# Ending the dense expert steps ahead of the first slot transposes in a two-layer kernel

## The chip, the cores and the metric

The kernel runs on one core of one Trainium2 chip. The metric is the device time of one execution in microseconds (us). A core has TensorE (matrix products), VectorE, ScalarE, GpSimd and SyncE (issues DMAs), each with its own stream of instructions, which meet in semaphores. In the rows PE is TensorE, DVE is VectorE, ACT is ScalarE, POOL is GpSimd, SP is SyncE.

## The reference, cut to what matters

Two layers, each with an attention block and a mixture of experts, are applied to 16 x 64 tokens of 128 channels. The change lies in the last block, the experts of the second layer: 1024 tokens, 8 experts of width 512, the two best experts for each token:

```python
logits = xf @ router_w.T
top_vals, top_idx = jax.lax.top_k(logits, TOP_K)          # TOP_K = 2, E = 8
gate = jax.nn.softmax(top_vals)
comb = zeros((N, E)).at[arange(N)[:, None], top_idx].add(gate)
for e in range(E):
    h = jax.nn.gelu(xf @ w1[e].T, approximate=False)
    out = out + comb[:, e:e + 1] * (h @ w2[e].T)
```

## The kernel before

The kernel is written engine by engine, with semaphores set and awaited by hand; each engine runs its instructions in the order written. In the experts of the second layer the first half of the tokens (512) is computed densely: every expert for every token, weighted afterwards. The second half is computed sparsely: each token's row is scattered by an indirect DMA of GpSimd into a DRAM buffer `slots_x`, sorted by expert, in 15 slots of 128 rows; the slots are read back in four batches (0: slots 0 to 2, 1: slots 3 to 6, then 7 to 10, 11 to 14), and each slot is multiplied with the weights of the one expert that owns it. Values are split in a high and a low 16-bit part, so that each product is made of three.

All of it is one loop of 47 steps (`STEPS`), n = 0 to 46. Steps 0 to 27 are dense (`DENSE` = 28: expert e = n // 4, quarter c = n % 4 of its width, for experts 0 to 6), steps 28 to 42 are the 15 slots, and 43 to 46 are the dense steps of expert 7. A step goes through five stages:

- up(n), on TensorE, into one of four PSUM banks: `up1` (lines 1585 to 1587, three products of 512 columns) for a dense step, `slot_up` (lines 1659 to 1661, four times three products of 128 columns) for a slot. The slot's expert is a register value, so the addresses of its weights are computed by register operations of TensorE.
- gelu(n) (line 782) and high(n) (line 787, the high part), on ScalarE: `gelu_step` and `high1_step`.
- low(n) (line 1208, the low part), on VectorE: `low1_step`.
- down(n), on TensorE: `down1` (lines 1606 to 1608, four times three products) or `slot_down` (lines 1678 and 1679, four times two).

TensorE computes up(n + 3) in the iteration of down(n). For n = 25 and above the four parts of a slot's up stand between the four parts of down. Every engine runs the loop in its own way: ScalarE does gelu(n + 1), then high(n); VectorE does low(n), then, at every fourth n, `add_expert` (line 1217), which weighs a finished dense expert's sum and adds it to the residual. add_expert(5) stands in iteration 24 and add_expert(6) in iteration 28. From iteration 29 on `result_row` (line 1231) takes the result of each slot, and GpSimd scatters it to `slots_y` (line 587).

Before a slot's up, its rows have to be turned: `transpose_slots(b)` (line 1640) has TensorE transpose a batch into PSUM bank 5, two 128 x 128 pieces a slot, once the batch has been read (`in_slots[b]`), and `copy_slots(b)` (line 1225) has VectorE copy that to `xsT`. `slot_up_waits(i)` waits for that copy. The table `FETCH` says in which iteration both stand: batch 0 in 24, batch 1 in 27, batch 2 in 31, batch 3 in 35. In the rows the tile `xsT` and the result rows go by the name of the buffer that holds them, `kM`; the slots' rows as read are in `kS`, and the hidden values are in `attention_or_experts`.

Of the kernel before, what the change touches and what calls it, by code (L numbers as in the profile page):

```python
# [43 lines left out]
FC = 4  # L44
# [11 lines left out]
SLOTS = 15  # L56
ROW = 264
AFTER = FC
DENSE = X1 * FC - AFTER
STEPS = DENSE + SLOTS + AFTER  # L60
FETCH = {DENSE - 4: 0, DENSE - 1: 1, DENSE + 3: 2, DENSE + 7: 3}

PACK = {}
_at = 0
# [7 lines left out]
def build_program(nc, x, ctx_t, ctx_v, pack, rows, w_first, w_second, qkvo, causal, ident_h, ident_b, sel_first, sel_second, out):  # L72
    with ExitStack() as stack:
# [178 lines left out]
        def reached(count):  # L252

            return max(count, 0) if type(count) is int else count
# [43 lines left out]
        def up_bank(n):  # L298

            return bank((3, 2, 0, 1)[n % 4])  # L300
# [38 lines left out]
        def gt(g):  # L339
            return slice(g * TG, (g + 1) * TG)  # L340
# [251 lines left out]
        def _(a):  # L592
# [48 lines left out]
            for c in range(4):  # L641
# [4 lines left out]
                n = min(4, NB - 1 - 4 * c)  # L646
# [132 lines left out]
            def gelu_step(n):  # L779

                a.wait_ge(s["mm1b"], n + 1)
                a.activation(up_bank(n), up_bank(n), ACT.Gelu, scale=1 / (XS * XS)).then_inc(s["gelu"], 1)  # L782

            def high1_step(n):
                a.wait_ge(s["gelu"], n + 1)
                a.wait_ge(s["mm2b"], reached(n - 3))
                a.activation(ehi[:, n % 4, :], up_bank(n), ACT.Copy, scale=HS).then_inc(s["hhi1"], 1)  # L787

            gelu_step(0)
            for n in range(STEPS):  # L790
                if n + 1 < STEPS:
                    gelu_step(n + 1)
                high1_step(n)
                if n < 2:
                    copy_pT(7, n)
                if n == 1:
                    gate_tanh(0)
                if n == 3:
                    copy_two_oT()
                if n == 5:  # L800
                    copy_oT(7)
                if n == 11:
                    copy_xT(3, 1, 5)
                if n == 12:
                    a.wait_ge(s["s1"], NT)
                    a.activation(xrow[:, :, :, 0:P], xn[:, gt(1), :].unsqueeze(2).to_broadcast([P, TG, 2, P]), ACT.Copy, scale=XS)\
                        .then_inc(s["rows_hi"], 1)
                if n == 16:
                    gate_tanh(1)
# [10 lines left out]
        def _(v):  # L820
# [413 lines left out]
            for n in range(STEPS):  # L1234
# [33 lines left out]
                if n == 22:  # L1268
                    place_gates()
                if n in FETCH:  # L1270
                    copy_slots(FETCH[n])
            def add_slots(k, t):
# [15 lines left out]
        def _(pe):  # L1288
# [92 lines left out]
            for g in range(G):  # L1381

                pe.wait_ge(s["cT_ready"], g + 1)
                for t in range(TG):
                    for pair in range(2):
                        for hf in range(2):
                            b = 2 * (g * TG + t) + hf
                            c = (2 * t + pair) * P + hf * S
# [266 lines left out]
            def slot_up(i, e, c):  # L1655

                o = up_bank(DENSE + i)[:, c * P:(c + 1) * P]
                high, low = of_expert(e, c, 0), of_expert(e, c, 1)
                mm(o, high, xsT[:, i, 0, :], start=True, stop=False)  # L1659
                mm(o, high, xsT[:, i, 1, :], start=False, stop=False)  # L1660
                last = mm(o, low, xsT[:, i, 0, :], start=False, stop=True)
                if c == FC - 1:
                    last.then_inc(s["mm1b"], 1)
# [60 lines left out]
            for n in range(STEPS):  # L1724
                if n == 0:
                    transpose_values(5)
                    pe.wait_ge(s["rdiff"], 1)
                if n == 1:
                    weighted_values(7)
                if n == 2:  # L1730
                    transpose_values(6)
                if n == 4:
                    output_product(5)
                    output_product(6)
                    transpose_values(7)
                if n == 6:
                    output_product(7)
                if n == 17:
                    owner = owners()
                if n in FETCH:  # L1740
                    transpose_slots(FETCH[n])
                m = n + 3
                if m < DENSE or DENSE + SLOTS <= m < STEPS:
                    up1(m)
                elif m < DENSE + SLOTS:
                    slot_up_waits(m - DENSE)
                    slot_up(m - DENSE, owner[m - DENSE], 0)
                if n == 10:
                    pe.wait_ge(s["x_att"], NT)
                    transpose_norm(3, 1, 5)  # L1750
                if n == 12:
                    router(3, 1, 1, X1, "router_w")
                if n == 14:
                    ranks()
                slots_down = DENSE <= n < DENSE + SLOTS
                if slots_down:
                    slot_down_waits(n - DENSE)
                else:
                    down1_waits(n)
                for c in range(FC):  # L1760
                    if slots_down:
                        slot_down(n - DENSE, owner[n - DENSE], c)
                    else:
                        down1(n, c)
                    if DENSE <= m < DENSE + SLOTS and c + 1 < FC:
                        slot_up(m - DENSE, owner[m - DENSE], c + 1)


# [92 lines left out]
```

## Time and profile before

| | us |
|---|---|
| median of 3 runs | 243.71 (243.09 to 244.08) |
| profiled execution, own time | 241.5 |
| its span, first to last instruction | 239.7 |
| busy TensorE | 206.5 (86%) |
| busy VectorE | 178.4 (74%) |
| busy ScalarE | 139.7 (58%) |
| mean granted TensorE clock | 0.984 |

The durations used below come from the one profiled execution, so sums are made against its span of 239.7 us and its own time of 241.5 us. Times in rows are us from the span's start. A busy share is an average over stages with different limits; which wait ends last at one place is seen only in the rows of that place.

### The profile page before, as it was taken

Reading aid. Unit: us, or ns where it says so; the run is one execution under the profiler, and the core shown is the slowest. Engines: PE = TensorE matmul, PEld = TensorE weight load, DVE = VectorE, ACT = ScalarE, POOL = GpSimd, SP = SyncE. Lnnn points to the kernel's source line nnn. Section 1 sums busy time; section 2 is a strip of 40 time slices with the busy share of each in tenths; the row PEclk is TensorE's granted clock in tenths of the full one; section 3 lists DMA queues with packets and bytes.
Section 4 is the critical chain, followed back from the end, with each engine's and each line's share of the span. In section 5 each row is a group of like instructions: output and inputs, shape, how many; then the busy total and the mean of one; then the engine's idle time right before and its main releaser. Section 6 shows DMA issues by size and latency. Waiting matters only on the chain.

```text
span 239.7 us, 6285 instructions
## 1 busy us (share of the span) xinstructions
PE 206.5 (86%) x2226; PEld 142.0 (59%) x2226; DVE 178.4 (74%) x476; ACT 139.7 (58%) x240; POOL 145.5 (61%) x184
## 2 busy tenths in 40 slices
PE   8979999769799999697678889999975879999990
PEld 2435679343355565345466776787763648777760
DVE  6665628959978888875995985579799585776675
ACT  2051354858654554505799988776773565566660
POOL 8646891150698877847799995770585730254550
PEclk9999999997999999979999999999999999999999
DMA  6920445001011210291100030022000125001115
GB/s 209 398 73 3 119 103 159 6 0 34 4 33 37 66 33 0 57 287 16 71 3 3 4 90 5 0 90 90 0 4 0 59 68 138 14 33 36 47 49 172
DMA packets 12891, 15.66 MB, mean 65 GB/s; under 512 B 1744, under 2 KB 9808, under 8 KB 12736
## 3 DMA queue, kind: packets, MB, share of 16 engines
q1 hardware_dynamic: 10448, 12.64, 17.6%
q0 software_dynamic: 736, 1.53, 1.9%
q10 hardware_dynamic: 1680, 1.13, 1.5%
q8 instruction: 17, 0.28, 0.5%
q14 instruction: 10, 0.08, 0.1%
HBM read 11.18 MB, written 3.06 MB: 59 GB/s over the span
## 4 chain that ended last, share of the span: by engine, by line
PE 58%; DVE 14%; issue 8%; ACT 7%; DMA 6%; POOL 4%; SPq 1%; POOLq 0%; DVEq 0%; ACTq 0%
PE ps L1678 4%; DMA attention_or_experts<-ctx_v 4%; PE ps L1295 3%; PE ps L1442 3%; PE ps L1557 3%; PE ps L1537 3%; PE ps L1444 3%; PE ps L1443 3%; POOL slots_x L582 3%; PE ps L1459 2%; PE ps L1357 2%; PE ps L1585 2%; PE ps L1587 2%; PE ps L1586 2%; PE ps L1659 2%
## 5 line engine op out<-in xcount | busy, mean ns | idle before, releaser
L782 ACT ACTIVATE ps<-ps 128x512 f32<-128x512 f32 x47 | 27.4, 584 | 26.8 <-PE ps L1587 16.2
L1208 DVE SCALAR_TENSOR_TENSOR attention_or_experts<-ps,attention_or_experts 128x512 f16<-128x512 f32 x47 | 31.9, 686 | 13.8 <-ACT attention_or_experts L787 13.7
L587 POOL DMA_INDIRECT slots_y<-kM,kS x15 | 14.3, 953 | 23.8 <-DVE kM L1231 22.6
L787 ACT ACTIVATE attention_or_experts<-ps 128x512 f16<-128x512 f32 x47 | 27.7, 593 | 0.0
L1295 PE MATMUL ps<-idle 128*128 128x512 f16 x82 | 23.4, 441 | 3.8 <-ACT kT L618 1.6
L1606 PE MATMUL ps<-keys_or_scores,attention_or_experts 128*128 128x128 f16 x128 | 23.5, 219 | 3.5 <-issue 2.6
L1608 PE MATMUL ps<-keys_or_scores,attention_or_experts 128*128 128x128 f16 x128 | 23.5, 219 | 0.0
L1607 PE MATMUL ps<-keys_or_scores,attention_or_experts 128*128 128x128 f16 x128 | 23.5, 219 | 0.0
L412 POOL TENSOR_TENSOR rstd<-ve,minus_half 128x4 f32<-128x4 f32 x8 | 8.3, 1039 | 22.2 <-DVE ve L839 22.1
L681 ACT ACTIVATE attention_or_experts<-ps 128x512 f32<-128x512 f32 x18 | 10.7, 597 | 18.9 <-PE ps L1444 18.9
L483 POOL TENSOR_TENSOR keys_or_scores<-kT,keys_or_scores 128x512 f16<-128x512 f32 x16 | 18.5, 1155 | 2.4
L1295 PEld LDWEIGHTS ps<-idle 128*128 128x128 f16 x82 | 8.8, 113 | 15.9 <-issue 5.7
L1606 PEld LDWEIGHTS ps<-keys_or_scores,attention_or_experts 128*128 128x128 f16 x128 | 12.6, 98 | 8.0 <-issue 5.8
L980 DVE TENSOR_TENSOR attention_or_experts<-attention_or_experts,ps 128x512 f32<-128x512 f32 x18 | 12.3, 686 | 5.5 <-ACT attention_or_experts L681 5.5
L1678 PE MATMUL ps<-keys_or_scores,attention_or_experts 128*128 x60 | 15.8, 279 | 0.1
L1459 PE MATMUL ps<-wsp,attention_or_experts 128*128 128x128 f16 x72 | 13.0, 220 | 2.7 <-DVE attention_or_experts L991 2.7
L1442 PE MATMUL ps<-xhi,wsp 128*128 128x512 f16 x36 | 14.4, 400 | 0.6 <-issue 0.4
L553 POOL TENSOR_TENSOR attention_or_experts<-attention_or_experts 128x1024 f16<-128x1024 f32 x6 | 12.9, 2157 | 2.7 <-ACT attention_or_experts L734 2.2
L476 POOL TENSOR_SCALAR kT<-raw 128x512 f32<-128x512 f32 x16 | 9.9, 617 | 7.6 <-DVE xn L846 3.7
L1443 PE MATMUL ps<-xlo,wsp 128*128 128x512 f16 x36 | 14.4, 399 | 0.0
L603 ACT ACTIVATE xT<-ps 128x512 f32<-128x512 f32 x8 | 4.8, 597 | 16.4 <-PE ps L1306 16.4
L1444 PE MATMUL ps<-xhi,wsp 128*128 128x512 f16 x36 | 14.2, 395 | 0.0
(255 smaller groups left out, 690.5 us busy)
## 6 DMA issues: line engine op xcount, KB each, us to landing
raw<-w_second SPq DMA_DIRECT2D x5, 512.0 KB, 3.6
raw<-w_first SPq DMA_DIRECT2D x9, 192.0 KB, 2.4
raw<-w_second SPq DMA_DIRECT2D x6, 256.0 KB, 3.0
attention_or_experts<-ctx_v SPq DMA_DIRECT2D x1, 1056.0 KB, 9.7
slots_x<-kS SPq DMA_DIRECT2D x1, 990.0 KB, 7.2
kS<-slots_x SPq DMA_DIRECT2D x3, 264.0 KB, 3.4
rw<-rows ACTq DMA_DIRECT2D x1, 512.0 KB, 7.1
ctxT<-ctx_t SPq DMA_DIRECT2D x1, 512.0 KB, 7.1
```

Of the source, the lines that this page charges most:

```text
L483: pool.tensor_tensor(low, raws[:, c].rearrange("p (c m) -> p c m", m=P), high, ALU.subtract).then_inc(s["wsp1_ready"], 1)
L782: a.activation(up_bank(n), up_bank(n), ACT.Gelu, scale=1 / (XS * XS)).then_inc(s["gelu"], 1)
L787: a.activation(ehi[:, n % 4, :], up_bank(n), ACT.Copy, scale=HS).then_inc(s["hhi1"], 1)
L1208: v.scalar_tensor_tensor(elo[:, n % 4, :], up_bank(n), HS, ehi[:, n % 4, :], ALU.mult, ALU.subtract)\
L1295: mm(bank(b), idle[:, 0:P], idle[:], start=True, stop=True)
L1442: mm(bank(2 * i + k), wsp[:, p, 0, c], xhi[:, tok(g)], start=True, stop=False)
L1443: mm(bank(2 * i + k), wsp[:, p, 0, c], xlo[:, tok(g)], start=False, stop=False)
L1444: last = mm(bank(2 * i + k), wsp[:, p, 1, c], xhi[:, tok(g)], start=False, stop=True)
L1606: mm(o, ehi[:, n % 4, ts], we[:, e, FC + c, 0, :], start=(c == 0 and t == 0), stop=False, skip_group_check=True)
L1607: mm(o, ehi[:, n % 4, ts], we[:, e, FC + c, 1, :], start=False, stop=False, skip_group_check=True)
L1608: last = mm(o, elo[:, n % 4, ts], we[:, e, FC + c, 0, :], start=False, stop=(c == FC - 1), skip_group_check=True)
L1678: mm(o[:, 0:2 * P], ehi[:, n % 4, cs], both, start=(c == 0), stop=False, skip_group_check=True)
```

## The change

TensorE no longer mixes the ups of slots 0 to 2 with the downs of steps 25 to 27. All dense steps run first, up(27) and down(24) to down(27), then the transposes of batch 0, then the ups of slots 0, 1 and 2 one behind the other, and in iteration 28 the transposes of batch 1 with the up of slot 3 right behind them. VectorE's copies follow the table: batch 0's from iteration 24 to 27, batch 1's from 27 to 28. On ScalarE high(27) now stands ahead of gelu(28).

```diff
-FETCH = {DENSE - 4: 0, DENSE - 1: 1, DENSE + 3: 2, DENSE + 7: 3}
+FETCH = {DENSE - 1: 0, DENSE: 1, DENSE + 3: 2, DENSE + 7: 3}
...
             for n in range(STEPS):
-                if n + 1 < STEPS:
+                if n == DENSE - 1:
+                    high1_step(n)
                     gelu_step(n + 1)
-                high1_step(n)
+                else:
+                    if n + 1 < STEPS:
+                        gelu_step(n + 1)
+                    high1_step(n)
...
-                if n in FETCH:
+                if n >= DENSE and n in FETCH:
                     transpose_slots(FETCH[n])
                 m = n + 3
                 if m < DENSE or DENSE + SLOTS <= m < STEPS:
                     up1(m)
-                elif m < DENSE + SLOTS:
+                elif DENSE + 3 <= m < DENSE + SLOTS:
                     slot_up_waits(m - DENSE)
                     slot_up(m - DENSE, owner[m - DENSE], 0)
...
-                    if DENSE <= m < DENSE + SLOTS and c + 1 < FC:
+                    if DENSE + 3 <= m < DENSE + SLOTS and c + 1 < FC:
                         slot_up(m - DENSE, owner[m - DENSE], c + 1)
+                if n == DENSE - 1:
+                    transpose_slots(FETCH[n])
+                    for i in range(3):
+                        slot_up_waits(i)
+                        for c in range(FC):
+                            slot_up(i, owner[i], c)
```

The order on TensorE around the transposes of batch 0, before (`in_slots0` is the DMA of that batch, `hlo1` counts VectorE's low parts; the rows ahead are the end of down(23)):

```order
L1608 MATMUL ps<-keys_or_scores,attention_or_experts 128x128
L1640 MATMUL ps<-idh,kS 128x128 [waits xsT_ready,in_slots0]
L1640 MATMUL ps<-idh,kS 128x128 x5
L1585 MATMUL ps<-xhi,keys_or_scores 128x512 [waits wsp1_ready,hlo1]
L1586 MATMUL ps<-xlo,keys_or_scores 128x512
L1587 MATMUL ps<-xhi,keys_or_scores 128x512
L1606 MATMUL ps<-keys_or_scores,attention_or_experts 128x128 [waits yacc,hlo1,wsp1_ready]
```

And now, with lines shifted by 4 (the row ahead is the end of down(27); ISA is a register operation, `xsT_ready` counts VectorE's copies of batches):

```order
L1612 MATMUL ps<-keys_or_scores,attention_or_experts 128x128
L1644 MATMUL ps<-idh,kS 128x128 [waits xsT_ready,in_slots0]
L1644 MATMUL ps<-idh,kS 128x128 x5
L1663 ISA [waits hlo1,wsp1_ready,xsT_ready]
L1663 MATMUL ps<-kM,keys_or_scores 128x128
L1664 MATMUL ps<-kM,keys_or_scores 128x128
L1665 ISA
L1665 MATMUL ps<-kM,keys_or_scores 128x128
```

Between the transposes and the first slot's up, which waits for their copy, stood up(27) and down(24); now nothing stands there. The transposes of batch 1, further on in the changed program, on TensorE (the rows ahead end the up of slot 2, those behind are slot 3's up and the first down product of slot 0):

```order
L1665 MATMUL ps<-kM,keys_or_scores 128x128
L1644 MATMUL ps<-idh,kS 128x128 [waits xsT_ready,in_slots1]
L1644 MATMUL ps<-idh,kS 128x128 x7
L1663 ISA [waits hlo1,xsT_ready]
L1663 MATMUL ps<-kM,keys_or_scores 128x128
L1664 MATMUL ps<-kM,keys_or_scores 128x128
L1665 ISA
L1665 MATMUL ps<-kM,keys_or_scores 128x128
L1682 ISA [waits y_ready,yacc,hlo1]
L1682 MATMUL ps<-keys_or_scores,attention_or_experts 128x256
```

Before, the slot's up that followed the transposes of batch 1 was slot 2's, which needs only batch 0. On VectorE, before, from add_expert(5) to add_expert(6) (the copies of three and of four slots are the COPY rows):

```order
L1217 SCALAR_TENSOR_TENSOR xr<-ps,gate,xr 128x128 x3
L1225 COPY kM<-ps 128x768 [waits xsTp]
L1208 SCALAR_TENSOR_TENSOR attention_or_experts<-ps,attention_or_experts 128x512 [waits mm2b,hhi1] x3
L1225 COPY kM<-ps 128x1024 [waits xsTp]
L1208 SCALAR_TENSOR_TENSOR attention_or_experts<-ps,attention_or_experts 128x512 [waits mm2b,hhi1]
L1217 SCALAR_TENSOR_TENSOR xr<-ps,gate,xr 128x128 [waits yacc,gate1_ready,mm2b]
```

And the same stretch of VectorE now:

```order
L1221 SCALAR_TENSOR_TENSOR xr<-ps,gate,xr 128x128 x3
L1212 SCALAR_TENSOR_TENSOR attention_or_experts<-ps,attention_or_experts 128x512 [waits mm2b,hhi1] x3
L1229 COPY kM<-ps 128x768 [waits xsTp]
L1212 SCALAR_TENSOR_TENSOR attention_or_experts<-ps,attention_or_experts 128x512 [waits mm2b,hhi1]
L1221 SCALAR_TENSOR_TENSOR xr<-ps,gate,xr 128x128 [waits yacc,gate1_ready,mm2b]
L1221 SCALAR_TENSOR_TENSOR xr<-ps,gate,xr 128x128 x3
L1229 COPY kM<-ps 128x1024 [waits xsTp]
```

The three low parts of steps 25 to 27 moved ahead of the first copy, and low(28) with add_expert(6) moved ahead of the second.

## Rows read from the trace of the kernel before

**Rows 1.** The chain of work that ended last: start us, us, what.

```profile
195.54 2.46 DMA kS<-slots_x
198.05 0.51 PE ps L1640 x6
...
215.43 0.28 PE ps L1678
```

**Rows 2.** Timeline: start us, us, engine, line; brackets: idle before, its releaser.

```profile
196.27 0.22 PE L1608 MATMUL ps<-keys_or_scores,attention_or_experts 128*128 128x128 f16 x1
196.52 1.12 DVE L1217 SCALAR_TENSOR_TENSOR xr<-ps,gate,xr 128x128 f32<-128x128 f32 x4 [0.42 <-PE ps L1608]
```

**Rows 3.** Timeline from 198 to 200.5 us.

```profile
198.05 0.51 PE L1640 MATMUL ps<-idh,kS 128*128 128x128 f16 x6 [1.57 <-DMA kS<-slots_x]
198.40 0.38 PE L1585 MATMUL ps<-xhi,keys_or_scores 128*128 128x512 f16 x1
198.60 0.56 DVE L1225 COPY kM<-ps 128x768 f16<-128x768 f16 x1 [0.95 <-PE ps L1640]
...
199.04 0.22 PE L1606 MATMUL ps<-keys_or_scores,attention_or_experts 128*128 128x128 f16 x1
199.07 0.68 DVE L1208 SCALAR_TENSOR_TENSOR attention_or_experts<-ps,attention_or_experts 128x512 f16<-128x512 f32 x1
...
199.24 0.58 ACT L782 ACTIVATE ps<-ps 128x512 f32<-128x512 f32 x1 [2.58 <-PE ps L1587]
...
199.74 0.59 ACT L787 ACTIVATE attention_or_experts<-ps 128x512 f16<-128x512 f32 x1
...
200.36 0.69 DVE L1208 SCALAR_TENSOR_TENSOR attention_or_experts<-ps,attention_or_experts 128x512 f16<-128x512 f32 x1 [0.61 <-ACT attention_or_experts L787]
```

**Rows 4.** Timeline from 202.4 us to slot 3's up and VectorE behind it.

```profile
202.48 0.61 PE L1640 MATMUL ps<-idh,kS 128*128 128x128 f16 x8
...
202.93 0.22 PE L1659 MATMUL ps<-kM,keys_or_scores 128*128 128x128 f16 x1
...
203.13 0.69 DVE L1225 COPY kM<-ps 128x1024 f16<-128x1024 f16 x1 [0.22 <-PE ps L1640]
...
203.74 0.68 DVE L1208 SCALAR_TENSOR_TENSOR attention_or_experts<-ps,attention_or_experts 128x512 f16<-128x512 f32 x1
...
204.27 0.22 PE L1659 MATMUL ps<-kM,keys_or_scores 128*128 128x128 f16 x1
...
204.47 0.61 DVE L1217 SCALAR_TENSOR_TENSOR xr<-ps,gate,xr 128x128 f32<-128x128 f32 x2
...
205.51 0.68 DVE L1208 SCALAR_TENSOR_TENSOR attention_or_experts<-ps,attention_or_experts 128x512 f16<-128x512 f32 x1
```

**Rows 5.** Timeline of the last dense steps, VectorE and TensorE.

```profile
231.88 1.29 DVE L1208 SCALAR_TENSOR_TENSOR attention_or_experts<-ps,attention_or_experts 128x512 f16<-128x512 f32 x2 [0.61 <-ACT attention_or_experts L787]
...
232.72 0.22 PE L1606 MATMUL ps<-keys_or_scores,attention_or_experts 128*128 128x128 f16 x1 [0.48 <-DVE attention_or_experts L1208]
```

**Rows 6.** Line 1678's register operations (ns min/median/max); timeline inside the slot stage.

```profile
L1678 PEldq FUSED_REGOPS  x60: 46/46/46, 204.5 to 229.2; - x60
...
212.56 0.69 DVE L1208 SCALAR_TENSOR_TENSOR attention_or_experts<-ps,attention_or_experts 128x512 f16<-128x512 f32 x1 [0.46 <-ACT attention_or_experts L787]
...
213.47 0.23 PE L1661 MATMUL ps<-kM,keys_or_scores 128*128 128x128 f16 x1
213.71 0.28 PE L1678 MATMUL ps<-keys_or_scores,attention_or_experts 128*128 x1
...
214.08 0.28 PE L1678 MATMUL ps<-keys_or_scores,attention_or_experts 128*128 x1
```

**Rows 7.** Stretches: us, busy of each engine (instructions), PEclk, DMA share, GB/s.

```profile
98.00:102.00 4.00, 1.73 (x26) 1.28 (x24) 3.09 (x5) 2.51 (x4) 3.54 (x6) 1.00 0.39 91
...
103.00:105.00 2.00, 2.00 (x6) 0.64 (x5) 1.33 (x8) 0.00 (x0) 1.02 (x1) 0.50 1.21 298
...
182.00:187.00 5.00, 1.19 (x15) 0.87 (x15) 4.61 (x18) 1.09 (x2) 2.44 (x4) 1.00 0.04 14
```

## Prediction

> Names: up(n), gelu(n), high(n), low(n), down(n) are the stages of step n (TensorE, ScalarE, ScalarE, VectorE, TensorE); steps 0 to 27 are dense, 28 to 42 are slots 0 to 14, 43 to 46 the last dense ones. T0, T1 are the transposes of slot batches 0 (slots 0 to 2) and 1 (slots 3 to 6), C0, C1 VectorE's copies of them.
>
> **What bounds the kernel now.** I read the chain of work first. From 195.54 it runs through the reading back of batch 0 until T0 at 198.05; from there it stays on TensorE through the slots (215.43 is one of many such rows) [rows 1], and the last additions and the output follow the last down products. So what happens to TensorE between 196 and 205 us is passed on to the end. The timeline just ahead of T0 shows what the DMA costs: the last product of down(23) starts at 196.27, add_expert(5) at 196.52, and then nobody has work [rows 2]. T0 comes with an idle time of 1.57 us in front of it, released by the DMA. In the order now, up(27) stands behind T0 (198.40), and C0 (198.60) stands on VectorE ahead of low(25) (199.07), so the data's lateness holds low(25) up too [rows 3]. From 202.93 to 204.27 slot 2's up and down(27) take 24 products in 1.34 us, 0.056 us each; nothing waits, and slot 3's up starts at 204.27 [rows 4]. I use that start as the mark: behind it both programs issue the same instructions.
>
> **The change, step by step.** Nothing is computed more or less; only order changes. From rows: 0.64 us for three up products (198.40 to 199.04), 0.67 for twelve down products (12 x 0.056), 0.35 for T0 (198.05 to 198.40), 0.45 for T1 (202.48 to 202.93) [rows 3, 4]. Latencies: gelu starts 0.03 after its up's last product has ended (the third of up(27) starts two times 0.215 behind 198.40 and takes 0.38, so 199.21; 199.24), high starts 0.50 after its gelu (199.74) and takes 0.59, low begins 0.03 behind high (200.36) and takes 0.69 [rows 3]. TensorE starts 0.15 after the low it waits for (the first of the pair at 231.88, + 0.69 = 232.57; 232.72) [rows 5]. On VectorE add_expert starts 0.73 after the low before it (203.74, 204.47), and the next instruction 1.04 after that (205.51) [rows 4].
>
> 1. TensorE is free at 196.33. up(27) runs to 196.97, down(24) to 197.64 (low(24) stands ahead of the add_expert(5) that starts at 196.52 [rows 2], so it is done).
> 2. down(25) needs low(25). VectorE is in add_expert(5) until 196.52 + 1.04 = 197.56; low(25) ends at 198.25, down(25) runs 198.40 to 199.07: TensorE idles **0.76**.
> 3. up(27) ended at 197.14, gelu(27) starts at 197.17, high(26) at 197.67, low(26) at 198.29, ending at 198.98; down(26) 199.13 to 199.80 (idle **0.06**). low(27), right behind, is done by 199.67, so down(27) follows at once, to 200.47.
> 4. T0 is issued at 200.47. Its data landed at 198.05, so that wait is gone. But now nothing stands between T0 and the first slot's up: T0's products end 0.51 after their start, C0 takes 0.56 [rows 3], and slot 0's up starts at 200.98 + 0.04 + 0.56 + 0.15 = 201.73. TensorE idles **0.91**. Before, up(27) and down(24) covered this.
> 5. Three slots' ups in a row. Each product is 0.056, so 0.67 a slot from below. The trace of before has them only mixed with down products. With two register operations to six products no gap shows (1.34 for 24), but in the slot stage a group of five products with three register operations takes 0.37 (213.71 to 214.08), where the products need 0.34 (four of 0.056, one twice as wide), and each register operation is listed at 46 ns [rows 6]. A pure run has two to three products: 0.17 us a group if they are hidden. If instead TensorE's issuing sets the pace, the group of 0.37 is three times 46 ns and ten issues (a weight load and a product each) of 23 ns, an estimate from these rows, and a pure group is two times 46 and six times 23 ns, 0.23. That is 0.67 to 0.92 a slot; I take 0.80, between them, since the densest mixture seen shows a gap but a small one. Three slots: 2.40, **0.39** more than the 2.01 of products alone. They end at 204.13, and T1 at 204.58 (batch 1 was there at 202.48 already [rows 4]).
> 6. Slot 3's up needs C1. VectorE meets it only behind low(28) and add_expert(6). low(28) needs high(28), and ScalarE has gelu(29) ahead of that, which needs slot 1's up: its last product ends at 201.73 + 1.60 + 0.16 = 203.49. So gelu(29) 203.52, high(28) 204.02 to 204.61, low(28) from 204.64, add_expert(6) from 205.37, C1 from 206.41; a copy of four slots takes 0.69 [rows 4]. It ends at 207.10, and slot 3's up starts at 207.25. TensorE idles **2.67**. Before, C1 stood ahead of low(28), under down(27). What is queued behind TensorE's wait is slot_down(0) and thereby every later slot; nothing else is there to do, since all dense steps before slot 0 are used up.
>
> What is taken away is the gap from 196.33 to 198.05, **1.72**, and about **0.09** of small gaps in the mixed steps 25 and 26 (from down(24)'s end, 199.04 + 0.67 = 199.71, to T1 at 202.48 are 2.77 us, 48 products need 2.68). Sum: 0.76 + 0.06 + 0.91 + 0.39 + 2.67 - 1.72 - 0.09 = **+2.98 us**, as 207.25 against 204.27 says.
>
> Is it given back later? Each slot iteration takes about 1.72 us of TensorE (213.71 to 215.43 [rows 1, 6]). At 213.71 slot_down's first product starts 0.24 us after the up product ahead of it (213.47), though its low was done at 213.25 [rows 6]: TensorE's own issue sets this pace, not a wait. At the other end, the reading of the results and the output follow slot_down(14) and the last dense steps, so they shift with TensorE. The two loads on SyncE that follow batch 0 and the scatters on GpSimd don't depend on the moved work. I count nothing back.
>
> The profiled execution's own time is 241.5 at a span of 239.7; so the forecast is a span of 242.7, an own time of 244.5, and, added to the median of the runs shown (243.71, 2.2 above the profiled one), **246.7 us**. Only the ups' pace varies it much: at 0.67 for each, slot 3 starts at 206.99 (+2.72), at 0.92 at 207.49 (+3.22). With 0.3 for the latencies either way, 246.1 to 247.2. About 0.5% (1.2 us) is what a measurement of this kernel can tell from no change.
>
> **Rivals.**
> *The clock falls.* The granted clock was 0.50 from 103 to 105, behind four microseconds in which TensorE was busy for 1.73; but it stayed at 1.00 through 182 to 187, where it was busy for only 1.19 of 5 [rows 7]. In the new stretch 200.8 to 207.2 it is busy for about 2.9 of 6.4, more than in either, with one idle time of 2.67. If it fell behind the wait for C1 for as long as at 102 to 106, some 3.4 us at 1.2 instead of 2.4 GHz, 1.7 us more of product time would be needed: 248.4. The Trainium skill (TensorE: Matmul & The Clock Gate, "The HAM clock gate") says the throttled state is the default and activity releases it, which speaks against emptying TensorE's queue; whether this gap is enough the trace of before leaves open. Chance 0.12.
>
> *It is given back.* If 0.14 us of the 0.24 ahead of each slot_down were a wait for the chain gelu, high, low after all, a TensorE that comes late would find all of it done, and 15 iterations would return 15 x 0.14 = 2.1 us: 244.6, within the measurement's doubt. Against it: low is done 0.46 before its use [rows 6]. Chance 0.08.
>
> *Faster.* If none of the new waits were paid, TensorE's stream would be 196.33 + 0.64 + 2.68 + 0.35 + 2.40 + 0.45 = 202.85 at slot 3's up, 1.42 before 204.27: 242.3. It decides by C1: it would have to end by 202.7. As low(28) stands before it and cannot even start before slot 1's up is computed, this needs VectorE's queue to be other than its order. The 1.57 us in the profile invites it; the rest speaks against it. Chance 0.03.
>
> *Slower, but by another amount* (half of the C1 wait hidden in a way I don't see, or an added stall in instruction supply): 0.05, between 245.2 and 246.1 or above 247.2.
>
> **The numbers.** Forecast 0.72, clock 0.12, given back 0.08, faster 0.03, other 0.05. Slower by over 0.5%: 0.72 + 0.12 + 0.05 = 0.89; within: 0.08; faster: 0.03. The range goes from 245.2 (the low end of "other") to 248.4 (the clock's case).
>
> **What would show it.** T0 without a DMA wait, near 200.5; an idle TensorE of about 0.9 ahead of slot 0's up and 2.7 ahead of slot 3's, released by VectorE's copies; low(28) and add_expert(6) between C0 and C1; slot 3's up near 207.2; about 1.72 us a slot behind it; clock 1.00. Wrong would be: a slot stage with a shorter period, a wait for C1 under 1 us, or a clock of 0.5 near 207.

## The result and the profile after

The changed kernel takes **248.42 us** (median of 4 runs, 246.55 to 249.5) where the kernel before takes 243.40 (4 runs, 242.55 to 244.08) beside it. The ratio is **1.0186, 95% interval 1.0146 to 1.0226**: slower by 4.5 us, between 3.6 and 5.5 (the two medians are 5.0 apart). The forecast was a loss of 2.98 us, 246.7. Direction and place hold, the amount was too small, and the time lies on the upper end of the stated range (248.4), which had been set by the clock's case and not by what made up the difference. The profiled execution took 248.87 us, with a span of 247.1. Some executions of most kernels here have a lower mean granted clock and are one to four per cent longer; the ratios leave them out, the medians don't.

Three lines of the page of the profile after: its head, the busy time of each engine, and the granted clock in 40 slices of the span.

```profile
span 247.1 us, 6285 instructions
...
PE 212.1 (86%) x2226; PEld 147.2 (60%) x2226; DVE 178.3 (72%) x476; ACT 140.1 (57%) x240; POOL 145.6 (59%) x184
...
PEclk9999999977999999999978899999997999799999
```

TensorE's share of the span is the same 86% as before, in a longer span, so this page shows no cause. The mean granted clock is 0.958 where the profiled execution of before had 0.984; more on that below. The place shows in the timeline after, in the same columns as [rows 3, 4]:

```profile
199.72 0.38 PE L1589 MATMUL ps<-xhi,keys_or_scores 128*128 128x512 f16 x1
199.90 1.48 SPq L389 DMA_DIRECT2D kS<-slots_x  x3
199.92 1.13 DVE L1221 SCALAR_TENSOR_TENSOR xr<-ps,gate,xr 128x128 f32<-128x128 f32 x4 [0.40 <-PE ps L1612]
...
201.79 0.22 PE L1610 MATMUL ps<-keys_or_scores,attention_or_experts 128*128 128x128 f16 x1 [0.59 <-DVE attention_or_experts L1212]
...
203.86 0.50 PE L1644 MATMUL ps<-idh,kS 128*128 128x128 f16 x6
204.39 0.56 DVE L1229 COPY kM<-ps 128x768 f16<-128x768 f16 x1 [1.42 <-PE ps L1644]
205.09 0.23 PE L1663 MATMUL ps<-kM,keys_or_scores 128*128 128x128 f16 x1 [0.74 <-DVE kM L1229]
...
208.03 0.23 PE L1663 MATMUL ps<-kM,keys_or_scores 128*128 128x128 f16 x1
208.27 0.23 PE L1663 MATMUL ps<-kM,keys_or_scores 128*128 128x128 f16 x1
...
208.53 0.61 PE L1644 MATMUL ps<-idh,kS 128*128 128x128 f16 x8
208.64 0.69 DVE L1212 SCALAR_TENSOR_TENSOR attention_or_experts<-ps,attention_or_experts 128x512 f16<-128x512 f32 x1 [3.69 <-ACT attention_or_experts L787]
209.25 1.12 DVE L1221 SCALAR_TENSOR_TENSOR xr<-ps,gate,xr 128x128 f32<-128x128 f32 x4
210.28 0.68 DVE L1229 COPY kM<-ps 128x1024 f16<-128x1024 f16 x1
211.10 0.23 PE L1663 MATMUL ps<-kM,keys_or_scores 128*128 128x128 f16 x1 [1.97 <-DVE kM L1229]
211.54 0.28 PE L1682 MATMUL ps<-keys_or_scores,attention_or_experts 128*128 x1
```

How to read it: up(27) starts at 199.72 behind down(23). SyncE issues its next three loads at 199.90, once batch 0 has landed; I call that time the landing (198.02 in the trace of [rows 3]). down(25) waits for low(25) until 201.79. T0 at 203.86 waits for no DMA, as its data is 3.96 us old. Slot 0's up waits for C0 until 205.09, and slot 3's up for C1 until 211.10, with low(28) (208.64) and add_expert(6) (209.25) between C0 and C1 on VectorE. TensorE had nothing between 209.0 and 211.1.

The sizes that matter are distances in one trace, since the executions differ in what happened to them earlier. From up(27) to slot 3's up, TensorE's products and transposes need 6.13 us in either program (0.64 + 0.35 + 2.68 + 0.45 + 2.01, by [rows 3, 4]); the rest are gaps:

| us | before, its profile | forecast | after |
|---|---|---|---|
| TensorE free for up(27) | 196.33 | 196.33 | 199.72 |
| slot 3's up | 204.27 | 207.25 | 211.10 |
| distance | 7.94 | 10.92 | 11.38 |
| less 6.13: gaps | 1.81 | 4.79 | 5.25 |

From there to the last slot_down are 25.19 us where before had 24.69 (first product of slot_down(0) at 211.54, and at 204.56): nothing is given back.

### The profile page after: what moved, and what is told of

It is laid out like the page before. It is cut to its first block, busy times and chain, and to the rows that moved or that the text cites. A ratio compares the mean times of both kernels' runs of the same rounds, so it can differ in the third digit from the quotient of the medians.

```text
span 247.1 us, 6285 instructions
## 1 busy us (share of the span) xinstructions
PE 212.1 (86%) x2226; PEld 147.2 (60%) x2226; DVE 178.3 (72%) x476; ACT 140.1 (57%) x240; POOL 145.6 (59%) x184
## 4 chain that ended last, share of the span: by engine, by line
PE 59%; DVE 18%; issue 9%; ACT 6%; DMA 4%; POOL 2%; SPq 1%; DVEq 0%; POOLq 0%; ACTq 0%
PE ps L1682 4%; DMA attention_or_experts<-ctx_v 4%; PE ps L1541 3%; PE ps L1446 3%; PE ps L1561 3%; PE ps L1448 3%; PE ps L1447 3%; PE ps L1589 2%; PE ps L1610 2%; PE ps L1590 2%; PE ps L1591 2%; PE ps L1612 2%; PE ps L1611 2%; PE ps L1663 2%; PE ps L1361 2%
## 5 line engine op out<-in xcount | busy, mean ns | idle before, releaser
L1299 PE MATMUL ps<-idle 128*128 128x512 f16 x82 | 20.7, 402 | 3.8 <-ACT kT L618 1.7
L1682 PE MATMUL ps<-keys_or_scores,attention_or_experts 128*128 x60 | 16.4, 290 | 0.2
L1299 PEld LDWEIGHTS ps<-idle 128*128 128x128 f16 x82 | 8.1, 104 | 13.9 <-ACT kT L618 2.5
L1663 PE MATMUL ps<-kM,keys_or_scores 128*128 128x128 f16 x60 | 13.8, 231 | 2.8 <-DVE kM L1229 2.7
```

The lines of the kernel that those rows point to most:

```text
L1299: mm(bank(b), idle[:, 0:P], idle[:], start=True, stop=True)
L1682: mm(o[:, 0:2 * P], ehi[:, n % 4, cs], both, start=(c == 0), stop=False, skip_group_check=True)
```

## The experiments

One row of each trace carries most of what follows, so it stands here once. The landing is as above; "slot_down(0)" is the start of its first product; us of each trace's own span. Where T0 doesn't wait for the DMA, the last column also holds how early or late TensorE came, so it compares two kernels only if TensorE came alike.

| kernel | landing | T0 | slot 0's up | T1 | slot 3's up | slot_down(0) | landing to slot_down(0) |
|---|---|---|---|---|---|---|---|
| before, its profile | 198.02 | 198.05 | 199.71 | 202.48 | 204.27 | 204.56 | 6.54 |
| before, repeated | 197.98 | 198.01 | 199.85 | 202.96 | 204.78 | 205.04 | 7.06 |
| after | 199.90 | 203.86 | 205.09 | 208.53 | 211.10 | 211.54 | 11.64 |
| T1 late alone | 199.35 | 199.56 | 201.50 | 206.46 | 208.52 | 208.94 | 9.59 |
| T1, C1 early | 197.18 | 201.20 | 202.88 | 202.44 | 206.09 | 206.96 | 9.78 |
| fixed weights | 199.12 | 203.09 | 204.24 | 206.26 | 209.37 | 209.74 | 10.62 |
| kept warm | 199.86 | 203.88 | 205.11 | 208.44 | 210.96 | 211.32 | 11.46 |
| fill the wait | 198.14 | 200.32 | 201.74 | 204.23 | 206.01 | 206.31 | 8.17 |

**Is it the wait for C1? T1 late alone.** The kernel before, with batch 1 one iteration later and nothing else:

```diff
-FETCH = {DENSE - 4: 0, DENSE - 1: 1, DENSE + 3: 2, DENSE + 7: 3}
+FETCH = {DENSE - 4: 0, DENSE: 1, DENSE + 3: 2, DENSE + 7: 3}
```

> The kernel before with one part of the change alone: T1 and C1 in iteration 28 in place of 27; T0, C0 and the mixed ups of slots 0 to 2 stay. C1 stands behind low(28) and add_expert(6). low(28) can start at 203.63 (high(28) ends there), add_expert(6) at 204.36, C1 at 205.40, slot 3's up at 206.24 in place of 204.27: +2.0 us, ratio 1.008, if the clock stays; +3.6 us, 1.015, if it falls in the gap of 1.8 us that this opens. Rival (C1's place costs nothing while the pipeline is full): 1.000 to 1.002.

Measured: 245.59 us (10 runs), ratio **1.0071 (1.0023 to 1.012)**. The timeline of this kernel:

```profile
206.46 0.61 PE L1640 MATMUL ps<-idh,kS 128*128 128x128 f16 x8
...
206.66 1.13 DVE L1217 SCALAR_TENSOR_TENSOR xr<-ps,gate,xr 128x128 f32<-128x128 f32 x4 [0.16 <-PE ps L1608]
...
207.70 0.68 DVE L1225 COPY kM<-ps 128x1024 f16<-128x1024 f16 x1
...
208.52 0.23 PE L1659 MATMUL ps<-kM,keys_or_scores 128*128 128x128 f16 x1 [1.46 <-DVE kM L1225]
```

TensorE idles 1.46 us for a copy that stands behind an add_expert, as in the changed kernel, though ups and downs are still mixed. T0 to slot 3's up is 8.96, 2.19 more than in the repeated run of before (6.77). This part of the mechanism is shown by itself, and costs some 0.7%.

**What if it is taken out of the change? T1, C1 early.** The changed kernel with T1 right behind T0 and C1 right behind C0:

```diff
-                if n >= DENSE and n in FETCH:
+                if n > DENSE and n in FETCH:
                     transpose_slots(FETCH[n])
...
                 if n == DENSE - 1:
-                    transpose_slots(FETCH[n])
+                    transpose_slots(0)
+                    transpose_slots(1)
...
-                if n in FETCH:
+                if n in FETCH and n != DENSE:
                     copy_slots(FETCH[n])
+                if n == DENSE - 1:
+                    copy_slots(1)
```

> The changed kernel with the transposes of batch 1 (T1) right behind those of batch 0 on TensorE and both copies (C0, C1) one behind the other on VectorE, ahead of low(28) and add_expert(6). The changed kernel stands at 1.0186 of before (+4.5 us). Theory of the order (C1 late behind low(28) and add_expert(6), and the clock falls because of the gap that this opens): the wait of 1.97 us ahead of slot 3's up shrinks to a wait of about 0.7 us of slot_down(0) for low(28), about 1.5 us come back, and with the clock staying at 1.0 near 210 another 1.6: about +1.4 us on before, ratio 1.006. Order matters but the clock falls anyway: +3.0 us, 1.012. Rival (the emptied pipeline as such costs the time, wherever C1 stands): 1.016 to 1.019.

Measured: 246.65 us (before 243.28 in the same series, 19 runs), ratio 1.015 (1.0029 to 1.027), an interval too wide to tell it from the changed kernel by time. The timeline of this kernel, slot 3's up and slot_down(0):

```profile
206.09 0.23 PE L1665 MATMUL ps<-kM,keys_or_scores 128*128 128x128 f16 x1
...
206.96 0.28 PE L1684 MATMUL ps<-keys_or_scores,attention_or_experts 128*128 x1 [0.52 <-DVE attention_or_experts L1212]
```

Nothing waits ahead of slot 3's up; the wait of 0.74 for C0 stands ahead of T1 now, which comes before slot 0's up. T0 to slot_down(0) fell from 7.68 to 5.76, by 1.92 where 1.5 was expected, and the granted clock stays at 1.00 behind it. Of the 2.1 us of idle time 0.52 come back a few instructions later: slot_down(0) now meets low(28), which the wait for C1 had hidden. Removing one wait exposes the next one on the same engine. The ratio of 1.006 that was expected is missed by the median. Of the 4.70 us that the change costs by distance, as worked out below, 2.8 are left without these 1.92, a ratio of some 1.011; the interval holds that, but the rival's 1.016 too.

**How dear are ups in a row? Fixed weights.** The changed kernel, in which the ups of slots 0 to 2 take expert 0's weights at fixed addresses instead of the owner's by register operations (so these three slots are computed with the wrong expert):

```diff
             def of_expert(e, c, k):
+                if e is None:
+                    return we[:, 0, c, k, :]
...
                         for c in range(FC):
-                            slot_up(i, owner[i], c)
+                            slot_up(i, None, c)
```

> The changed kernel with the ups of slots 0 to 2 on the weights of expert 0, at addresses fixed when the program is built (so these three slots are computed with the wrong expert, work and shapes unchanged). Theory that the register operations set the pace of the pure ups: 36 products in 2.0 to 2.1 us in place of 3.44, slot 3's up about 0.9 us earlier against T0. Rival (loading weights without down products in between sets it): 3.3 us or more, as before.

Stretches of the two traces from slot 0's up to T1 (columns of [rows 7]), the changed kernel's first:

```profile
205.09:208.53 3.44, 3.38 (x37) 2.54 (x38) 0.00 (x0) 1.59 (x3) 0.00 (x0) 1.00 0.02 5
```

```profile
204.24:206.26 2.02, 2.02 (x36) 2.02 (x37) 0.00 (x0) 1.05 (x2) 0.00 (x0) 1.00 0.00 0
```

And the timeline of the kernel with fixed weights at slot 3's up:

```profile
209.37 0.23 PE L1665 MATMUL ps<-kM,keys_or_scores 128*128 128x128 f16 x1 [2.50 <-DVE kM L1229]
```

36 products take 3.44 us with addresses from registers, 0.287 a group of three, and 2.02 with fixed ones, 0.168 a group, which is 0.056 a product. The granted clock is 1.00 in both. So the 1.42 us between them comes with the register operations, which nothing hides in a pure run. The 0.287 is a mean: the groups of the changed kernel start by turns 0.25 and 0.29 to 0.40 apart (205.09, 205.34, 205.74, 205.99, 206.34 and so on), those with fixed addresses 0.16 to 0.18. Why by turns no run shows. TensorE's row of busy time hides this (3.38 of 3.44), since the modelled ends of short products overlap the gaps; the distances of starts show it. Of the 1.42 us, T0 to slot 3's up gained 0.96 (6.28 against 7.24): the wait for C1 grew from 1.97 to 2.50 in exchange, as C1 still stands behind the same work on VectorE.

**Does the clock matter? Kept warm.** The granted clock fell right behind the wait for C1 in the trace after. Idle products on a spare bank, three ahead of slot 0's up and nine behind T1, fill both waits:

```diff
+                    if n == DENSE:
+                        keep_warm(7, 9)
...
                     transpose_slots(FETCH[n])
+                    keep_warm(7, 3)
                     for i in range(3):
```

> The changed kernel with products on an idle tile, written to a free PSUM bank, in TensorE's two waits: 3 of 512 columns ahead of slot 0's up (0.65 us into a wait of 0.74) and 9 behind T1 (1.94 us into a wait of 1.97). Theory of the clock: the fall to 0.5 from about 212.7 to 216 doesn't come and some 1.6 us are given back: +2.9 us on before, ratio 1.012. Rival (the clock's fall costs nothing because something else sets the pace there): 1.018 to 1.020 with the clock at 1.0.

The changed kernel's stretches behind slot 3's up, then those of the one kept warm:

```profile
212.00:213.00 1.00, 1.00 (x13) 0.85 (x13) 0.00 (x0) 0.03 (x1) 0.00 (x0) 0.76 0.00 0
213.00:216.00 3.00, 3.00 (x26) 2.75 (x25) 1.26 (x3) 1.53 (x3) 0.95 (x1) 0.51 0.00 0
216.00:218.00 2.00, 2.00 (x35) 1.94 (x33) 1.61 (x4) 1.49 (x4) 0.96 (x1) 1.00 0.13 41
```

```profile
213.00:216.00 3.00, 2.99 (x36) 2.35 (x35) 1.92 (x4) 1.80 (x4) 1.22 (x2) 1.00 0.09 27
```

With the wait filled the clock stays at 1.00, where it was 0.51 (1.2 GHz), behind a wait of 1.97. The slot stage, from slot_down(0) to the last one, then takes 24.60 us instead of 25.19: by this pair the fall costs **0.6 us**, a third of the 1.7 that the forecast gave this rival. In the traces of this document in which the clock doesn't fall there the stage takes 24.60 to 24.89, so 0.3 to 0.6 is what is known. In 213 to 216 the slow clock is felt in full, with 26 products instead of 36, and slot 2's down comes 0.95 later (4.39 against 3.44 us behind slot_down(0)). By slot 4 only 0.44 of it is left (7.77 against 7.33). What gives the rest back no run shows. The four runs of this kernel are 247.83 and 249.06 us, among those of the changed kernel (246.55 to 249.50), and 253.38 and 254.07 with mean clocks of 0.939 and 0.932; no gain in time is shown.

**A version that fills the wait.** up(27) and down(24) ahead of T0, down(25) and slot 0's up behind it, and the rest mixed as before:

```diff
-FETCH = {DENSE - 4: 0, DENSE - 1: 1, DENSE + 3: 2, DENSE + 7: 3}
+FETCH = {DENSE - 3: 0, DENSE - 1: 1, DENSE + 3: 2, DENSE + 7: 3}
...
+                if n == DENSE - 4:
+                    transpose_slots(0)
+                if m == DENSE:
+                    slot_up_waits(0)
+                    for c in range(FC):
+                        slot_up(0, owner[0], c)
```

> A gentler form of the change: up(27) and down(24) run ahead of T0, down(25) runs between T0 and slot 0's up, slot 0's up is pure, and the ups of slots 1 and 2 stay mixed with down(26) and down(27); T1 and C1 stay in iteration 27, ahead of low(28); C0 moves behind low(25). By the rows of before: T0 at 198.05, down(25) 198.40 to 199.07, C0 done 199.2, slot 0's up 199.3 to 200.4 (at 0.29 us a group as the changed kernel shows), then 1.35, T1 0.45, 1.35: slot 3's up at 203.5 against 204.27. Ratio 0.997 (-0.8 us), at most 0.995. Rival (leaving the full mixture costs as much as the filled DMA wait gives): 1.000 or above.

Measured: 243.56 us (10 runs), ratio 1.0028 (0.9981 to 1.0075): no gain is shown. T0 is issued 2.18 us behind the landing, so in this execution there was no DMA wait to fill. That called for a second look at the kernel before.

**The kernel before, repeated.**

> The kernel before, unchanged, once more with a profile. Of 19 other executions of it 14 have a mean granted clock of 0.959 to 0.968, while the profile on which the prediction rests has 0.984. Theory of the untypical profile: in a usual execution the clock falls to 0.5 from about 187 us, behind TensorE's wait of some 3 us for the slots' owners, TensorE reaches T0 about 1.5 us later against the landing of batch 0, and the wait of 1.57 us for the DMA ahead of T0 is at most 0.3 us; from the landing to slot_down(0) are then about 7.4 us instead of 6.54. Rival (the profile was typical there): no fall near 187, a wait of 1.3 to 1.6 us ahead of T0, 6.5 us to slot_down(0).

242.39 us, span 240.6, clock 0.975. Its timeline at the landing, T0 and slot 3's up, and then its stretches:

```profile
197.98 1.48 SPq L389 DMA_DIRECT2D kS<-slots_x  x3
198.01 0.51 PE L1640 MATMUL ps<-idh,kS 128*128 128x128 f16 x6
...
204.78 0.22 PE L1659 MATMUL ps<-kM,keys_or_scores 128*128 128x128 f16 x1
```

```profile
188.00:190.00 2.00, 2.00 (x13) 1.18 (x12) 0.69 (x1) 0.66 (x2) 1.49 (x2) 0.50 0.20 68
190.00:192.00 2.00, 2.00 (x23) 1.65 (x22) 0.69 (x1) 1.24 (x3) 1.39 (x2) 0.80 0.15 42
```

T0 has no bracket: the 1.57 us of [rows 3] are gone. Where the profile that the forecast rests on had 22 products at a clock of 1.00 in 188 to 190, this execution has 13 at 0.50. The clock had fallen behind the same long idle time, which in the trace of the forecast reads so, its timeline and then its stretch of 188 to 190:

```profile
184.69 0.22 PE L1606 MATMUL ps<-keys_or_scores,attention_or_experts 128*128 128x128 f16 x1 [2.60 <-issue]
```

```profile
188.00:190.00 2.00, 2.00 (x22) 1.30 (x20) 0.69 (x1) 1.74 (x4) 1.49 (x2) 1.00 0.20 68
```

The same row and the last product of down(23) in the repeated run, and then the row in the trace after:

```profile
184.68 0.22 PE L1606 MATMUL ps<-keys_or_scores,attention_or_experts 128*128 128x128 f16 x1 [2.60 <-issue]
...
197.86 0.22 PE L1608 MATMUL ps<-keys_or_scores,attention_or_experts 128*128 128x128 f16 x1
```

```profile
186.48 0.22 PE L1610 MATMUL ps<-keys_or_scores,attention_or_experts 128*128 128x128 f16 x1 [2.60 <-issue]
```

The two executions of before run alike up to this row (184.69 and 184.68). Behind it TensorE is free for T0 at 196.33 in the first and at 197.92 in the second, 1.6 us later, while the landing stays at 198.0. So TensorE is late by about as much as the DMA, and the wait isn't there to be removed. The trace after has the same fall, 0.50 from 189 to 192: from its row to TensorE's being free for up(27) are 13.24 us, as many as in the repeated run, where the trace of the forecast has 11.64. So the repeated run and the trace after are a fair pair. Every trace shown so far but that of the forecast has the fall, somewhere between 185 and 193. A mean clock of 0.984 was rare: of 19 other runs of this kernel 14 have 0.959 to 0.968, the other five less (the repeated run has 0.975). The forecast was made from an untypical execution.

**Can that state be made?** Idle products ahead of `down1_waits(16)`, under the wait at 184.69, in all three kernels (before, after, and the version that fills the wait):

```diff
                 else:
+                    if n == 16:
+                        keep_warm(5, 11)
                     down1_waits(n)
```

A first try put twelve of them ahead of `owners()` in iteration 17, which ran behind the wait, not in it, as the timeline of before with this edit shows:

```profile
192.47 2.75 PE L1295 MATMUL ps<-idle 128*128 128x512 f16 x12
```

> The kernel before with 12 products of 512 columns on an idle tile (2.6 us, into PSUM bank 5, free there) ahead of TensorE's reading of the slots' owners in iteration 17, where it waits about 3 us. Theory of the untypical profile: the clock stays at 1.0 around 187, TensorE comes to T0 some 1.5 us early and finds the wait for the DMA of 1.57 us; the end moves by only 0.7 to 0.9 us, since batch 0's landing sets it: ratio 0.997. Rival (the usual execution does not lose anything at 187): 1.000 and no change of the wait ahead of T0.

> The changed kernel with the same 12 products in iteration 17. The state around T0 is then that of the profile of before on which the prediction rests. Theory of the untypical profile: against the kernel of the previous label the cost is what the prediction says, +2.98, plus about 1.0 for the slower ups (1.15 us a slot as the changed kernel showed, against 0.80), +4.0 in from-landing-to-slot_down(0), 10.5 us against 6.5; ratio to before about 1.012 to 1.014. Rival (the loss of the change has nothing to do with when TensorE arrives): the ratio stays at 1.0186.

> The gentle form (up(27), down(24), T0, down(25), then slot 0's up) with the same 12 products in iteration 17. If the clock is kept up at 187, TensorE arrives early and has 1.57 us of DMA wait to fill: slot_down(0) comes 5.8 to 6.2 us behind the landing against 6.54, and the ratio to before is 0.994 (0.9 for the clock, 0.5 for the filled wait). Rival (the fill costs more by the pure up and the later C0 than it gives): slot_down(0) at 6.6 or more, ratio 0.997 or above.

Before with it: 246.97 us, ratio 1.0065 (1.0013 to 1.0117), so twelve products there cost 0.65%. After: 248.52 (4 runs); the filling version: 247.71 (4 runs). Landing to slot_down(0) is 6.50, 12.85 and 6.64; in the second TensorE came to up(27) 1.06 behind the landing. The edit missed its wait, so the times say nothing on the question. With the products in the right place:

> The kernel before with 11 products of 512 columns on an idle tile ahead of down(16), where TensorE really waits some 2.7 us (for low(16), which stands on VectorE behind the placing of the rows; the products of iteration 17 had come after this wait). The repeated profile of before has the clock at 0.5 behind this wait and TensorE at T0 without any wait, 7.06 us from landing to slot_down(0). Expected if the clock's state decides when TensorE arrives: clock 1.0 from 184 to 196, the DMA wait ahead of T0 back at 1.3 to 1.6 us, 6.5 us from landing to slot_down(0), ratio 0.997 to 0.999. Rival (the fall behind the wait doesn't move T0): no DMA wait, 7.0 us.

> The changed kernel with the same 11 products ahead of down(16). Expected if the prediction's sum holds in the state that it was read from: TensorE is free for up(27) about 1.7 us before the landing; from there to slot 3's up 11.0 to 11.4 us (predicted 10.9; the ups take 1.15 a slot instead of 0.80), so slot 3's up is 9.3 to 9.7 us behind the landing against 6.25 in the profile of before: +3.1 to +3.5 us, ratio to before 1.010 to 1.014. Rival (the change costs its 4.5 us in any state): ratio 1.018.

> The gentle form (up(27) and down(24) ahead of T0, down(25) between T0 and slot 0's up) with the same 11 products ahead of down(16). Its own trace had 6.0 us from T0 to slot_down(0); with TensorE early, T0 is at the landing, so 6.0 us from landing to slot_down(0) against 6.54: ratio 0.994 to 0.997, faster than both kernels. Rival (filling the wait is worth nothing): ratio 0.998 or above.

| with products ahead of `down1_waits(16)` | us (4 runs) | T0 | slot 3's up | landing to slot_down(0) |
|---|---|---|---|---|
| before | 244.98 (240.44 to 248.9) | 196.89 | 203.07 | 6.50 |
| after | 246.71 (245.08 to 251.28) | 206.11 | 213.34 | 10.13 |
| filling the wait | 245.47 (242.29 to 247.58) | 200.00 | 205.71 | 6.03 |

The kernel before with these products, its stretch of 188 to 190 and then its timeline at T0, and last T0 in the version that fills the wait:

```profile
188.00:190.00 2.00, 2.00 (x22) 1.31 (x20) 1.20 (x4) 1.76 (x4) 1.53 (x2) 1.00 0.22 70
```

```profile
196.89 0.51 PE L1640 MATMUL ps<-idh,kS 128*128 128x128 f16 x6 [1.70 <-DMA kS<-slots_x]
```

```profile
200.00 0.51 PE L1640 MATMUL ps<-idh,kS 128*128 128x128 f16 x6 [0.36 <-DMA kS<-slots_x]
```

The state of the forecast is back: clock 1.00, a DMA wait of 1.70, 6.50 us from the landing to slot_down(0) where the trace of the forecast has 6.54. TensorE comes 1.83 us ahead of the landing in before and 1.66 ahead of it in after, so here the distances from the landing compare: the changed kernel is slower by 3.63 us. Its distance from up(27) (free at 201.97) to slot 3's up is 11.37, as in the changed kernel (11.38). Its trace comes from its longest execution, 251.28 us with a mean clock of 0.949, but the clock is 1.00 from 185 to 213. Filling the wait brings 0.47 (6.03), as expected.

In time this is not confirmed. Against the kernel before without these products the changed kernel with them has a ratio of 1.0115 (1.0007 to 1.0223), but these products stand in one of the two only. With these products in both, the runs with a mean clock above 0.96 are 240.44 and 242.54 us before, 245.08, 245.66 and 247.76 after, and 242.29 and 243.97 in the filling version. Between the means of the first two are 4.7 us, from two and three runs. A gain of 0.5 from filling the wait can't be seen in runs that spread like this. No version that beats the kernel before is shown.

## Why the prediction came out as it did

The mechanism was right, and the sum was off in two of its terms. The yardstick is the table of gaps above, with the repeated run of before as the usual state: its distance from TensorE's being free (197.92) to slot 3's up (204.78) is 6.86, so 0.73 of gaps.

- **Step 2, the wait for low(25): right.** 0.75 measured, 0.76 forecast.
- **Step 4, the wait for C0: right.** 0.88 (start of slot 0's up behind T0 1.23, less 0.35) against 0.91. T0 waits for no DMA, as said.
- **Step 5, three ups in a row: mis-sized.** The term was 0.39, at 0.80 a slot; measured is 3.44 - 2.01 = **1.43**, 1.15 a slot, outside the 0.67 to 0.92 given. Both bounds were taken from mixed rows [rows 4, 6]; there, it seems, other products between the register operations hide them. The run with fixed weights shows that the register operations are the cause. What one costs when exposed was not in the trace before: 0.119 a group over 0.168, with two of them 0.060 each in the mean, more than the 46 ns in [rows 6].
- **Step 6, the wait for C1: right in place and cause, 2.12 against 2.67** (from T1's 0.45 to slot 3's up, 208.98 to 211.10). Of the 1.04 too little in step 5, 0.55 came back here. TensorE reaches this wait 1.04 later, counted from slot 0's up. low(28) needs slot 1's up but not slot 2's, so it starts only 0.64 later (3.55 against 2.91 behind slot 0's up), and from low(28) to slot 3's up are 2.46 instead of 2.61. T1 late alone shows the mechanism without the rest of the change.
- **What is taken away: the term that was furthest off.** The forecast took away 1.72 + 0.09 us of gaps from 196.33 on. In the usual state only 0.73 is there, 1.08 less, since TensorE arrives late after a fall of the clock at 187. The repeated run shows it; the kernels with products ahead of `down1_waits(16)` show that with the clock held the wait for the DMA returns (1.70), and that the changed kernel is then slower by 3.63 in distance. That it is then slower by less in time is not shown.
- **Is it given back: right, nothing is.** From slot_down(0) to the last the repeated run of before takes 24.89, after 25.19; with the clock kept, 24.60, within the spread of such traces.
- **The clock's rival, which had a chance of 0.12: came true beside the forecast, at a third of its price or less.** The clock was 0.51 from 213 to 216 behind the wait of 1.97. A clock of 0.5 there was one of the forecast's own signs of being wrong; the range reaches up to the measured time only by this rival's 1.7 us, of which 0.3 to 0.6 were real. That the time lies at its end is luck. It did not always fall: in the changed kernel with products in iteration 17 the same wait of 1.97 was followed by 1.00, and behind the 1.46 of T1 late alone it was 1.00 too. The timeline and then a stretch of the former:

```profile
210.52 0.23 PE L1663 MATMUL ps<-kM,keys_or_scores 128*128 128x128 f16 x1 [1.97 <-DVE kM L1229]
```

```profile
213.00:216.00 3.00, 2.95 (x38) 2.31 (x36) 1.81 (x3) 1.49 (x4) 1.57 (x2) 1.00 0.09 27
```

The sum, corrected: gaps of 5.25 less 0.73 are 4.52, and slot 3's up to slot_down(0) takes 0.44 instead of 0.26, so 4.70 at slot_down(0), with 0.3 to 0.6 for the clock in executions where it falls. Measured are 4.5 us (3.6 to 5.5). This rests on one trace of each kernel; the trace before repeated and the trace after are the pair that TensorE reached alike. Against the 2.98 of the forecast, 1.08 come from the gaps that weren't there and 0.46 from the new ones (5.25 instead of 4.79). The remaining distance between the two profiled spans, 247.1 and 239.7, lies ahead of the change: TensorE reached up(27) 3.39 us later in the trace after (199.72 against 196.33), in instructions that are alike in both programs. 1.60 of it comes with the fall from 188 to 192, and 1.79 stands already at 186.48; the trace after has two more stretches at 0.50, at 124 to 127 and 134 to 137, that the trace of the forecast hasn't. The exchange of high(27) and gelu(28) on ScalarE was not run by itself; the gaps of the other steps leave nothing for it.

## What to carry to other kernels

Products whose weight addresses come from registers were cheap here in a mixture: between products with fixed addresses nothing could be seen of them (24 products in 1.34 us), and in the slot stage, between slot_downs, it was 0.03 us for each group of five. In a pure run of slot_ups it was 0.119 us for each three. A copy that TensorE needs next must not stand behind work of VectorE that itself waits for TensorE's last results: that alone cost 0.7%. Before a wait in a profile is counted as removable, compare the mean clock of the profiled execution with that of the other runs; a wait that ends 10 us behind a fall of the clock can be there in one execution and not in the next.

## What was not expected of the hardware

- A stretch at 1.2 GHz cost 0.3 to 0.6 us over the slot stage (213 to 216; 25.19 against 24.60 to 24.89), though 26 products stood in it instead of 36. The Trainium skill (TensorE: Matmul & The Clock Gate, "The HAM clock gate") calls the throttled state the default that activity releases. By that rule this pair of traces agrees (0.51 behind an idle 1.97, 1.00 with the wait filled), but the same wait of 1.97 was also followed by 1.00.
- The same program, with the same idle time of 2.60 behind it, shows the clock at 1.00 in one execution and at 0.50 in the next. Which it is moved TensorE's arrival at the DMA wait 10 us later by 1.6 us, and with it the wait. No run here settles what decides it.
- Register operations of TensorE listed at 46 ns cost about 60 ns each in the mean when nothing hides them (1.42 us for 24 in 36 products).
